# Gated cross attention and a mixture-of-experts attention on one core: value matmuls of cross attention issued for eight heads at a time, with a ring of sixteen transposed blocks

## The reference, cut to what matters

```python
Qm, Km, Vm = ...                       # [32, 16, 100 or 361, 16]
scores = einsum('bhqd,bhkd->bhqk', Qm, Km) / sqrt(16)
scores = where(attn_mask, scores, fill)
attn = softmax(scores, axis=-1)
A = einsum('bhqk,bhkd->bhqd', attn, Vm)    # the value matmuls
O = einsum('bsd,ed->bse', A, Wo) + bo
x = x + tanh(g_xattn[0]) * O
```

## Time and profile before

| | |
|---|---|
| median of the runs | 1966.53 us |
| profiled execution | 1965.53 us |
| its span | 1963.7 us |
| TensorE busy over the span | 1885.1 us, 96% |
| VectorE busy | 1503.7 us, 77% |
| ScalarE busy | 1138.9 us, 58% |
| cross attention: first and last value matmul start | 77.8 and 592.4 us |

### The profile page before, as it was taken

How to read it: one execution, slowest core, us unless ns; L and a number is a source line. 1 busy time by engine, 2 the same in 40 slices (tenths; PEclk the granted TensorE clock), 3 DMA queues, 4 the chain that set the end, 5 groups by cost and what they waited for, 6 DMA issues and landing times. The chain is left out here.

```text
span 1963.7 us, 59110 instructions
## 1 busy us (share of the span) xinstructions
PE 1885.1 (96%) x13454; PEld 1154.2 (59%) x13454; DVE 1503.7 (77%) x4285; ACT 1138.9 (58%) x3588; POOL 933.8 (48%) x1361
## 2 busy tenths in 40 slices
PE   5899999999997999999999999959999999999998
PEld 2678888888875554444444444455555555555543
DVE  6688898888987943555555555538999999999989
ACT  3688888888885444444444444435555555555543
POOL 4122222222212003666666666626677766766767
PEclk9999999999998999999999999969999999999999
DMA  3777888788752483000000000063222222222202
GB/s 123 145 115 117 118 119 120 119 119 121 119 80 104 204 332 130 27 27 27 27 27 27 27 24 20 27 191 91 72 78 72 68 83 66 79 73 76 76 10 68
DMA packets 192136, 174.08 MB, mean 89 GB/s; under 512 B 51921, under 2 KB 183378, under 8 KB 190034
## 3 DMA queue, kind: packets, MB, share of 16 engines
q1 hardware_dynamic: 189906, 165.06, 37.0%
q0 software_dynamic: 2176, 8.39, 1.2%
HBM read 112.41 MB, written 60.98 MB: 88 GB/s over the span
## 5 line engine op out<-in xcount | busy, mean ns | idle before, releaser
L1442 POOL TENSOR_TENSOR o_side<-o_side,o_tmp 128x256 f32 (+1 forms) x528 | 398.4, 755 | 193.0 <-POOL o_side L1442 73.3
L1165 ACT ACTIVATE big<-e_pv,gates 128x128 f32<-128x128 f32 x800 | 228.7, 369 | 291.4 <-PE e_pv L1226 289.9
L640 ACT ACTIVATE c_ex<-c_sm,c_nmax 100x361 f32<-100x361 f32 x512 | 302.6, 593 | 55.5 <-DVE c_nmax L523 50.1
L1565 ACT ACTIVATE o_tmp<-o_py,gates 128x256 f32<-128x256 f32 x528 | 222.3, 475 | 191.9 <-PE o_py L1637 141.4
L1637 PE MATMUL o_py<-o_whi,a_chi 128*128 128x512 f16 x800 | 304.1, 380 | 0.4 <-DVE o_side L1498 0.2
L1226 PE MATMUL e_pv<-e_vhi,e_xhi 128*128 x800 | 303.2, 379 | 1.2 <-ACT e_out L1155 1.2
L1637 PE MATMUL o_py<-o_wlo,a_chi 128*128 128x512 f16 x800 | 303.5, 379 | 0.0
L1637 PE MATMUL o_py<-o_whi,a_clo 128*128 128x512 f16 x800 | 303.4, 379 | 0.0
L1226 PE MATMUL e_pv<-e_vlo,e_xhi 128*128 x800 | 303.2, 379 | 0.0
L1226 PE MATMUL e_pv<-e_vhi,e_xlo 128*128 x800 | 303.2, 379 | 0.0
L1104 DVE TENSOR_SCALAR e_acc<-e_pv,gates 128x128 f32<-128x128 f32 x400 | 121.8, 346 | 236.3 <-PE e_pv L1226 236.3
(11 more groups left out here) (166 smaller groups left out, 3392.4 us busy)
## 6 DMA issues: line engine op xcount, KB each, us to landing
qk<-e_out SPq DMA_DIRECT2D x16, 1600.0 KB, 5.2
c_kst<-k_parts SPq DMA_DIRECT2D x256, 90.2 KB, 4.9
a_q<-qk SPq DMA_DIRECT2D x64, 200.0 KB, 2.4
a_k<-qk SPq DMA_DIRECT2D x64, 200.0 KB, 2.5
v<-e_out SPq DMA_DIRECT2D x20, 640.0 KB, 3.3
a_v<-v SPq DMA_DIRECT2D x64, 200.0 KB
c_ctx<-in_ctx_t SPq DMA_DIRECT2D x32, 361.0 KB, 3.4
e_wst<-in_v_w POOLq DMA_DIRECT2D x8, 1024.0 KB, 7.8
```

The lines of the kernel that those rows point to most:

```text
L640: act.activation(ex[:, h % 4, 0:SK], sm[:, h % 4, :], ACT.Exp, scale=-1.0, bias=nmax[:, h % 4:h % 4 + 1], accum_out=den[:, b.par, HEAD[h]: ...
L1165: act.activation(tmp[:, hh, e, :], p_v[:, hh, 1, e * PD:(e + 1) * PD], ACT.Copy, scale=gate).then_inc(s_av, 1)
L1442: pool.tensor_tensor(side[:, x.t, :], side[:, x.t, :], tmp[:, slot(x, r), j, :], ALU.add).then_inc(s_pool, 1)
L1565: act.activation(tmp[:, slot(x, r), j, :], p_y[:, q, j, :], ACT.Copy, scale=gate).then_inc(s_av, 1)
```

## The change

The number of heads whose value matmuls are issued together is doubled, and with it the ring (`RING = 2 * CLOSE`, L316), from 8 blocks to 16 (from 9,600 to 19,200 bytes in each of 121 partitions).

```diff
@@ -33,7 +33,7 @@
 XH, XD = 16, 16
 XG = P // XD
 KC = 3
-CLOSE = 4
+CLOSE = 8
 HEAD = (0, 2, 4, 6, 1, 3, 5, 7, 8, 10, 12, 14, 9, 11, 13, 15)
 KW = -(-SK // KC)
 SKP = KC * KW
```

## The result

The changed kernel takes 1983.1 us (median of four runs, 1978.77 to 1983.44) against 1965.7 us for the kernel before (four runs): ratio 1.0085, 95% interval 1.0072 to 1.0098. It is slower, as forecast, and by 17 us where 8.2 were forecast.

What follows compares the result with a forecast made beforehand. A chain passing between TensorE, VectorE and ScalarE within each batch was taken as the bound. Terms +0.49 - 0.73 + 0.49 = +0.25 us a batch, times 31, plus 0.5 at the end, gave +8.2: 1974.6 us, range 1961 to 1984.

Steps and rivals of the forecast that it cites:

- rival C: Longer groups: 24 added matmuls cost 0.65 us each time, batch grows 0.57 us, 1985 us; chance 0.12.
- Part 1: Chain from the transposes at step 4 to those at step 8, 303.80 to 307.59, passing through TensorE and VectorE.
- part 3: Chain from the transposes of step 13 to the next step 4, 313.64 to 319.87, over ScalarE and VectorE.
- The price of 24 more matmuls: Value matmuls added to an existing group on TensorE: 24 x 20.5 ns, 0.49 us; ends 0.47 and 0.65.
- Step 4: Its group grows by 24 matmuls, wholly on the batch's chain: +0.49 us a batch.
- Step 12: Its group grows by 24 matmuls, and the later scores and transposes delay the chain: +0.49 us a batch.
- Step 0: Loses its group, but TensorE then waits for VectorE and ScalarE: 0 a batch, other end 0.74 us gained.
- Step 8: Loses its group, next scores come earlier and TensorE keeps the gain to step 12: -0.73 us a batch.
- The ring: Deepening it to sixteen blocks frees no copy and adds no new wait: 0.
- The later `s_pv`: At step 4 ScalarE's copy of the values starts perhaps 0.1 us late, but is covered: 0.
- Rival A: TensorE bounds every part, four fewer mode changes save 0.50 us a batch: 1950.5 us; chance 0.15.
- Rival B: Part of step 0's time comes back, 0.25 of 0.74 us, batch as long as before: 1967 us; chance 0.21.

Runs made afterwards that it cites:

- merge4: Kernel before with only heads 8 to 15 merged into one group at step 4, step 0's group gone, ring of sixteen; ratio 1.0071.
- less0: Kernel before, leaving out two of three key chunks of the value matmuls of heads 8 to 11 at step 0; ratio 1.0001.
- vfirst: Changed kernel with ScalarE's copy of the values' last chunk moved ahead of the exponential of head 9; 1977.97 us, 1.0064 to the kernel before.
- ring16: Kernel before with a ring of sixteen blocks and nothing else changed; ratio 0.9996.

## Why the prediction was right, and where its size was off

The measured 1983.1 us lies inside the range of 1961 to 1984 us, but at its edge, and nearer to rival C's 1985 than to my 1974.6. That the range held it is in part luck: a batch grew by 0.65 us, outside the 0.10 to 0.60 to which the ends of my terms added up. The direction and three of the four steps came as I had them; the size was off by one term.

**The chain in three parts.** Right. Part 1 grew by 0.52 us and part 3 stayed (+0.04).

**The price of 24 more matmuls, 0.49 us.** Right: the group of 48 has 47 spacings in 1.24 - 0.249 us, 21.1 ns each (20.5 before), and the scores come 1.17 us after its start (before 0.66): +0.51. Rival C's 0.65 is refuted, though its time of 1985 us was the closest: its 0.57 us a batch came from a dearer group and the full gain at step 8, the measured 0.65 from the group's price as I had it and a smaller gain.

**Step 4, +0.49.** Right: +0.52, and merge4 by itself gives +0.55 a batch, 0.7% of the time.

**Step 12, +0.49.** Right: 321.16 to 322.88 is 1.72 us, before 1.20 (311.79 to 312.99). Nothing absorbs it.

**Step 0, nothing given back.** Right, and shown twice: merge4 keeps the whole cost of step 4 although step 0's group is gone, and less0 wins nothing. The wait foreseen for step 1 is there.

**Step 8, -0.73.** This is the mis-sized term. The next scores do come 0.69 us earlier after the transposes (317.84 - 317.39 = 0.45 us, before 1.14), but only 0.43 us is left at step 12 (317.39 to 321.16 is 3.77 us, before 4.20, from 307.59 to 311.79). My sentence that "TensorE keeps the gain to step 12" looked at VectorE alone. ScalarE is the one in the way: 0.05 us are lost at step 9 (scores to scores 0.87 us, before 0.82), where the transposes wait for its copy, and 0.20 at step 11 (scores to keys 0.36 us, before 0.16), where the first keys' matmul writes the PSUM buffer that ScalarE's copy of the values' last chunk must have read (`keys`, L698, waits for `s_vz`). Before, TensorE was late enough there for this wait to be invisible: from 99 to 596 us no wait for `c_v` stands among its waits. vfirst takes it away and gets 0.21 us a batch back.

With the terms as measured, +0.52 + 0.52 - 0.43 + 0.04 = 0.65 us a batch, and 31 x 0.65 = 20 us. All four were read from one batch, so that they add up to its growth is no test. The test is the stage, which grew by 19.6 us (15.6 beside `ring16`), and the medians, which differ by 17.4.

**The ring, 0.** Right, by ring16.

**The later `s_pv`, 0.** Right in effect. ScalarE's copy of the values does wait for the longer group, 0.34 us at 315.04 in the batch above, but the exponential of head 6 behind it still waits for VectorE (0.19 us at 316.99), so the delay ends there.

**Rival A, the mode changes.** The row's 0.16 us after a group is real and two groups a batch are saved, but the time goes into waits. That TensorE counted as busy for 16.07 of 16.10 us says nothing of a limit: less0 takes 0.33 us of its work from each batch, it counts as busy for 16.05 of 16.08, and the time does not move. **Rival B**, part of step 0's time won, would have shown as a gain in less0; it has none.

## What to carry to other kernels

In a hand-written order over several engines, price a moved block of work by the step that it leaves and the step that it joins, not by its total: here the same merge costs 0.7% at one step and about 0.2% at another, and the step that loses work may give nothing back. Where a step is freed, walk every wait of every instruction that now comes earlier, waits on PSUM buffers of unrelated work included, for those that were hidden by the lateness just removed. A place at which growth costs in full and shrinking wins nothing is a tie; then look for the second limit before moving more there.

## What the runs showed of the hardware that was not expected

The group of 48 value matmuls runs at 21.1 ns an instruction with each one 249 ns long by its row, on four 32-column strips, and keeps that pace over twice the length. TensorE's busy share does not follow its work where matmuls are this short: 16 instructions fewer in a batch left it at 16.05 of 16.08 us. The other surprises were in the order of waits, and in the transfers, where reloads of the keys that start 3 us later cost 0.57 us in nearly every batch.
